# Attention and the later stages in one block, with the first two shared pairs between attention's last steps

## What is computed

```
h = h + attn(layernorm(h))          # gated attention unit: silu(x @ uv_w) -> u, v, q, k
                                    # relu(q k^T + w_rel)^2 @ v, times u, @ o_w, + x * res_scale
t = layernorm(h)
shared = sum over 2 experts of gelu(t @ sw1 + sb1) @ sw2, + sb2
cw     = softmax(t @ gate_w + gate_b), kept for the top 2 of 8 experts
routed = sum over 8 experts of cw * (gelu(t @ rw1 + rb1) @ rw2 + rb2)
out = h + shared + routed
```

## Time and profile before

| | us |
|---|---|
| median of three runs | 1364.53 |
| profiled execution | 1364.89 |
| its span | 1363.1 |
| TensorE busy | 1231.9 (90%) |
| VectorE busy | 1009.1 (74%) |
| GpSimd busy | 830.3 (61%) |
| ScalarE busy | 827.3 (61%) |

### The profile page before, as it was taken

How to read it: one execution, slowest core, us unless ns; L and a number is a source line. 1 busy time by engine, 2 the same in 40 slices (tenths; PEclk the granted TensorE clock), 3 DMA queues, 4 the chain that set the end, 5 groups by cost and what they waited for, 6 DMA issues and landing times.

```text
span 1363.1 us, 39403 instructions
## 1 busy us (share of the span) xinstructions
PE 1231.9 (90%) x11910; PEld 1010.8 (74%) x11911; DVE 1009.1 (74%) x2599; ACT 827.3 (61%) x1969; POOL 830.3 (61%) x824
## 2 busy tenths in 40 slices
PE   4999999999999998257999989999999999998997
PEld 2777877777777886235777778888888888966676
DVE  3688788778788787238777757777777777789997
ACT  1566566565656665153444447777777777756664
POOL 3345776676767765667777616676676676753331
PEclk7999999999999999668999999999999999999999
DMA  5233334343333312124444222222222322236663
GB/s 153 81 126 112 116 117 128 100 132 114 120 113 125 127 60 69 61 81 132 121 115 119 73 57 81 83 84 81 82 84 76 86 81 80 64 99 179 187 179 106
DMA packets 119520, 142.62 MB, mean 105 GB/s; under 512 B 18591, under 2 KB 98782, under 8 KB 119417
## 3 DMA queue, kind: packets, MB, share of 16 engines
q1 hardware_dynamic: 95800, 101.42, 25.6%
q0 software_dynamic: 19584, 33.45, 8.1%
q10 hardware_dynamic: 4032, 6.57, 1.9%
HBM read 86.38 MB, written 55.96 MB: 104 GB/s over the span
## 4 chain that ended last, share of the span: by engine, by line
PE 45%; DVE 7%; issue 3%; ACT 2%; DMA 0%; POOL 0%; DVEq 0%; ACTq 0%
PE bank L1615 4%; PE bank L1637 4%; PE bank L1636 4%; PE bank L1638 4%; PE bank L1616 4%; PE bank L1617 4%; PE bank L1081 3%; PE bank L1080 3%; PE bank L1079 3%; PE bank L1033 2%; PE bank L1034 2%; DVE hid_all L1062 2%; PE bank L1035 2%; DVE hid_all L1064 2%; PE bank L1603 2%
## 5 line engine op out<-in xcount | busy, mean ns | idle before, releaser
L1334 POOL DMA_INDIRECT y_dram<-y_sb,y_row x244 | 273.1, 1119 | 154.5 <-issue 74.5
L1041 ACT ACTIVATE gel_all<-bank,b 128x458 f32<-128x458 f32 x256 | 157.1, 641 | 161.8 <-PE bank L1035 148.5
L1411 ACT ACTIVATE gel_all<-bank,b 128x256 f32<-128x256 f32 x488 | 192.9, 473 | 54.1 <-PE bank L1617 30.3
L1081 PE MATMUL bank<-w_hi,hid_all 128*117 128x128 f16 (+1 forms) x1024 | 181.5, 221 | 0.0
L1080 PE MATMUL bank<-w_lo,hid_all 128*117 128x128 f16 (+1 forms) x1024 | 181.4, 221 | 0.0
L1079 PE MATMUL bank<-w_hi,hid_all 128*117 128x128 f16 (+1 forms) x1024 | 181.4, 221 | 0.0
L1636 PE MATMUL bank<-w_hi,hid_all 128*128 x976 | 173.1, 220 | 0.0
L1637 PE MATMUL bank<-w_lo,hid_all 128*128 x976 | 170.5, 219 | 0.0
L1638 PE MATMUL bank<-w_hi,hid_all 128*128 x976 | 170.5, 219 | 0.0
L1534 DVE CAST hid_all<-gel_all 128x1024 f16<-128x1024 f32 x122 | 85.4, 700 | 103.3 <-ACT gel_all L1411 103.3
L1323 POOL DMA_INDIRECT slots_dram<-rows_s,slot_2nd x128 | 133.6, 1044 | 39.6 <-issue 38.3
(11 more groups left out here) (185 smaller groups left out, 3266.8 us busy)
## 6 DMA issues: line engine op xcount, KB each, us to landing
xin<-in_xmain SPq DMA_DIRECT2D x32, 771.8 KB
rows_r<-slots_dram SPq DMA_DIRECT2D x122, 130.0 KB
x2r_dram<-rows_1st SPq DMA_DIRECT2D x32, 260.0 KB, 2.6
rows_s<-x2r_dram SPq DMA_DIRECT2D x32, 260.0 KB, 2.7
scratch<-y_dram SPq DMA_DIRECT2D x32, 234.0 KB
x2t_dram<-x2T SPq DMA_DIRECT2D x32, 229.0 KB, 2.9
scratch<-y_dram SPq DMA_DIRECT2D x32, 224.0 KB
x_cols<-x2t_dram ACTq DMA_DIRECT2D x28, 229.0 KB, 2.7
```

The source lines that it names most:

```text
L1081: last = pe.matmul(dst, lo, self.w_hi[:, w], start=False, stop=f == self.NG - 1)
L1334: pool.indirect_dma_start(out=y_dram, in_=y_sb[:, s, c, :], in_offset=None, out_offset=bass.IndirectOffsetOnAxis(ap=y_row[:, s, c:c + 1], ...
L1411: act.activation(gel[:, s8 % 2, f, :], up_bank[s8 % 2][half][:, (f % 2) * TILE:(f % 2 + 1) * TILE], ACT.Gelu, bias=b1[:, bass.ds((e + SHAR ...
```

## The change

Both functions now return their engines' programs and one block calls them, attention's first. All semaphores live to the end; `Done` hands attention's to the later stages. `ones`, `b2`, `x_cols`, `slot_1st` and the four row buffers are allocated outside both functions, and the buffers of the shared pairs lie over those of attention that are free by then.

After steps 30, 31 and 32 `steps` calls a function `between`. SyncE loads the columns of pairs 0 and 1 after step 30. After step 31 TensorE, ScalarE and VectorE do `up`, `gelu` and `split` of pair 0; after step 32, pair 1 with the `down` of pair 0. Pair 0 uses three PSUM banks in turn, and VectorE splits it like the others. The meeting of the engines and SyncE's waits between the blocks are gone; `load_rows(0)` to `(3)` wait for attention's scatter and store from the same buffer instead. `tag_rows` moves back by one pair (rows 2i-2 and 2i-1 in pair i), the fill tails go behind `load_rows(16)`, the tables are computed in three parts behind pairs 3, 4 and 5, and the memset of `scratch` goes from VectorE to GpSimd. The b2 work goes to attention's start: loads behind `rel`, sums and casts on GpSimd at the end of step -2. The experts' PSUM banks are renumbered.

```diff
-        def steps(eng, step):
+        def steps(eng, step, between=None):
...
             for i in range(hi, PAIRS + 4):
                 step(i, i % 2, i // 2, i % 4)
+                if between is not None and i >= PAIRS - 2:
+                    between(eng, i)
...
-            for parity in range(2):
-                sp.wait_ge(t_out[parity], 16 * PAIRS // 2)
-            for buf in range(ROW_BUFS):
-                sp.wait_ge(r_out[buf], 16 * PAIRS // ROW_BUFS)
-                sp.wait_ge(scattered[buf], 64 * PAIRS // ROW_BUFS)
-            sp.wait_ge(w_late, 16)
...
+            def sum_biases():
+
+                own = Own(pool, b2_up)
+                s0, s1 = EXPERTS * HID, (EXPERTS + 1) * HID
+                own.did(pool.memset(b2[:, :], 0.0))
+                pool.wait_ge(b2_loaded, 64)
+                own.did(pool.tensor_tensor(b2_in[:, s0:s1], b2_in[:, s0:s1], b2_in[:, s1:B2_COLS], ALU.add))
+                own.wait()
+                own.did(pool.tensor_copy(b2[0:B2_LO, :], b2_in[0:B2_LO, 0:s1]))
+                own.wait()
+                own.did(pool.tensor_copy(b2_high[B2_LO:, :], b2_in[B2_LO:, 0:s1]))
+                own.wait()
+                own.did(pool.tensor_tensor(b2[B2_LO:2 * B2_LO, :], b2_in[B2_LO:, 0:s1], b2_high[B2_LO:, :], ALU.subtract))
...
+                if isinstance(i, int) and i == -2:
+                    sum_biases()
...
+    def up_free(self, pe, k, f):
+
+        if self.before is not None and isinstance(k, int) and k < 2 and f < (3 if k == 0 else 4):
+            if k == 0:
+                pe.wait_ge(self.before.sil, 5 * PAIRS)
+            else:
+                pe.wait_ge(self.gel_ready, self.NG)
+                pe.wait_ge(self.before.mid_ready, PAIRS)
+        elif self.before is not None and isinstance(k, int) and k == 0:
+            pe.wait_ge(self.gel_ready, f - 2)
+        elif not (isinstance(k, int) and k == 0 and f < 4):
+            pe.wait_ge(self.gel_ready, self.NG * k + f - 3)
...
+        def sync_between(sp, i):
+            if i == PAIRS - 2:
+                for k in range(2):
+                    sp.wait_ge(done.t_out[k], 16)
+                    early.load(sp, k, k)
...
                 if i >= ROWS_BUFS:
                     sp.wait_ge(scattered[b], 64 * (i // ROWS_BUFS))
+                else:
+                    sp.wait_ge(done.scattered[b], 64 * PAIRS // ROW_BUFS)
+                    sp.wait_ge(done.r_out[b], 16 * PAIRS // ROW_BUFS)
...
             for i in range(PAIRS):
                 load_rows(i)
-                if i == 6:
+                if i == 16:
                     sp.wait_ge(tables_up, 3)
...
+            pool.memset(scratch[:, 1024:], 0.0).then_inc(scratch_up, 1)
...
+        def scalar_between(act, i):
+            if i == PAIRS - 1:
+                act.wait_ge(done.w_late, 16)
+                for f in range(NG):
+                    early.gelu(act, 0, f)
+                act.wait_ge(done.t_out[0], 32)
+                early.load(act, 2, 0)
+            if i == PAIRS:
+                for f in range(NG):
+                    early.gelu(act, 1, f)
+                act.wait_ge(done.t_out[1], 32)
+                early.load(act, 3, 1)
...
-                        tag_rows(2 * i, 2 * q % ROWS_BUFS)
+                        tag_rows(2 * i - 2, (2 * q + 2) % ROWS_BUFS)
...
             tag_rows(0, 0)
             tag_rows(1, 1)
-            for i in range(1, EARLY_PAIRS):
+            for i in range(2, EARLY_PAIRS):
...
+        def vector_between(dve, i):
+            if i == PAIRS - 1:
+                for j in range(NJ):
+                    early.split(dve, 0, 0, j)
+            if i == PAIRS:
+                vector_pair(dve, 1, 1)
...
+        def tensor_between(pe, i):
+            if i == PAIRS - 1:
+                pe.wait_ge(done.ws_done, PAIRS)
+                for f in range(NG):
+                    early.up(pe, 0, 0, f)
+            if i == PAIRS:
+                pe.wait_ge(done.b2_up, B2_STEPS)
+                tensor_pair(pe, 1, 1)
```

More of the change, by code:

```diff
@@ L15 @@
+from collections import namedtuple
 from contextlib import ExitStack
@@ L58 @@
 B2_LO = 32
+B2_COLS = (EXPERTS + SHARED) * HID
+B2_STEPS = 5
 EARLY_PAIRS = 18
@@ L72 @@
 TINY = 1e-30
+Done = namedtuple("Done", "t_out r_out scattered ws_done top_kept slots_up mid_ready sil x2T_ready routed lg_read w_late b2_up")
 class Own:
@@ new lines, in build @@
+        slot_1st = sbuf("slot_1st", [P, 2, GROUP], U32)
+        attend, done = embed_and_attend(
+            nc, keep, bank, acc, w_hi, w_lo, b1, ident, top8, slot_2nd, tag_2nd, region_at, next_at, ones, b2, row_bufs, slot_1st,
+            xmain, xrest, tokw_main, tokw_rest, txt, tokb, token, pos, emb2, emb3, emb4, w_rel, uv_w, o_w, gamma, beta, g, res,
+            gate_w, gate_b, ffn_w, ffn_b1, shared_b2, routed_b2, x2t_dram, x2r_dram, slots_dram)
+        experts = experts_and_combine(
+            nc, keep, done, bank, acc, w_hi, w_lo, b1, ident, top8, slot_2nd, tag_2nd, region_at, next_at, ones, b2, x_cols,
+            row_bufs, x2t_dram, x2r_dram, slots_dram, y_dram, out)
@@ new lines, in build, with _ @@
+        block = keep.enter_context(nc.Block())
+        @block.sync
+        def _(sp):
+            attend["sync"](sp, experts["sync_between"])
+            experts["sync"](sp)
+        @block.gpsimd
+        def _(pool):
+            attend["gpsimd"](pool)
+            experts["gpsimd"](pool)
+        @block.vector
+        def _(dve):
+            attend["vector"](dve, experts["vector_between"])
+            experts["vector"](dve)
+        @block.scalar
+        def _(act):
+            attend["scalar"](act, experts["scalar_between"])
+            experts["scalar"](act)
@@ L461, in _, with vector @@
             steps(pool, step)
-        @block.vector
-        def _(dve):
+        def vector(dve, between):
             own = Own(dve, setup_v)
@@ L701, in _, with scalar @@
                                      op0=ALU.mult, op1=ALU.subtract).then_inc(uvw_ready, 1)
-            steps(dve, step)
-        @block.scalar
-        def _(act):
+            steps(dve, step, between)
+        def scalar(act, between):
             act.wait_ge(w_in, 16 * N_W)
@@ L819, in step, with tensor @@
                     weights_hi(i, p)
-            steps(act, step)
-        @block.tensor
-        def _(pe):
+            steps(act, step, between)
+        def tensor(pe, between):
             def text(grp):
@@ L998, in _ @@
             pe.wait_ge(setup_v, 9)
-            steps(pe, step)
+            steps(pe, step, between)
+    done = Done(t_out, r_out, scattered, ws_done, top_kept, slots_up, mid_ready, sil, x2T_ready, routed, lg_read, w_late, b2_up)
+    return {"sync": sync, "gpsimd": gpsimd, "vector": vector, "scalar": scalar, "tensor": tensor}, done
 class SharedExperts:
@@ L1005, with __init__ @@
     NJ = NG // 2
-    def __init__(self, nc, ctx, tag, first, flip, bank, acc, w_hi, w_lo, b1, b2, ones, x_cols, gel, hid, x2t_dram):
+    def __init__(self, nc, keep, tag, first, flip, up_bank, down_bank, acc, w_hi, w_lo, b1, b2, ones, x_cols, gel, hid, x2t_dram,
+                 before=None):
         def sem(name):
-            return ctx.enter_context(nc.semaphore(f"{name}_{tag}"))
+            return keep.enter_context(nc.semaphore(f"{name}_{tag}"))
         self.first, self.flip, self.acc, self.x2t_dram = first, flip, acc, x2t_dram
@@ L1018, in __init__, with up_dst @@
         self.acc_done = sem("acc_done")
+    def up_dst(self, k, f):
+        lead = self.before is not None and isinstance(k, int) and k == 0
+        return self.up_bank[f % 3 if lead else f % 4][:, 0:PAIR_SEQ]
+    def up_free(self, pe, k, f):
[9 more added lines that the diff above has]
+            pe.wait_ge(self.gel_ready, self.NG * k + f - 3)
     def load(self, eng, k, parity):
@@ L1090, in accumulate, with experts_and_combine @@
                           ALU.add).then_inc(self.acc_done, 1)
-def experts_and_combine(nc, bank, acc, w_hi, w_lo, b1, ident, top8, slot_2nd, tag_2nd, region_at, next_at,
-                        shared_b2, routed_b2,
-                        x2t_dram, x2r_dram, slots_dram, y_dram, out):
+def experts_and_combine(nc, keep, done, bank, acc, w_hi, w_lo, b1, ident, top8, slot_2nd, tag_2nd, region_at, next_at, ones, b2,
+                        x_cols, row_bufs, x2t_dram, x2r_dram, slots_dram, y_dram, out):
     LAG, AHEAD = 2, 2
```

253 lines of the change are left out of this document (103 added, 150 removed).

## The result

The changed kernel takes 1354.11 us (median of 4: 1352.51, 1355.85, 1354.86, 1353.37), the kernel before 1364.57 (4 runs). The ratio is 0.9926, 95% interval 0.9909 to 0.9944. In a later comparison, with six runs, it was 1355.91 against 1365.00, ratio 0.9924 (0.9909 to 0.9939). Ratios and their intervals rest on the executions within 1.5% of a kernel's fastest; this leaves out only four of the twelve of experiment 4, the profiled one among them. The sign was right; the predicted 1341.0 and its range, 1334 to 1350, were not.

What follows compares the result with a forecast made beforehand. TensorE was taken as the bound after the seam's holes. Of its chain (transposes at 773.1) and GpSimd's (775.9), the later decides: against 799.67 a gain of 23.8, kept as 23.5, from 1364.53 to 1341.0 us, range 1334 to 1350.

Steps and rivals of the forecast that it cites:

- What bounds the kernel: Between attention and shared pairs, GpSimd's queue, a barrier and a load leave TensorE idle 24.23 us; afterwards TensorE is the bound.
- pair 0: First shared pair: up-projections start at 554.0 in an idle gap, delaying ScalarE's rows of pair 31 by 5 us to 563.4.
- pair 1 before rank(15): On TensorE pair 1 runs ahead of rank(15), ending at 581.4; slots are up at 583.3 where they were at 567.3.
- GpSimd to the first tag: Last first-choice scatters, fill and row loads put tags at 597.9; TensorE stops some 12 us before resuming near 600.0.
- Set-up: nothing: Bias work moved to the start takes GpSimd 7.6 us, delaying it 2.7, covered by 4.8 us before the first reader.
- Rival B: Row ring slips at load_rows(17) behind the fill tails: 1 to 2 us lost once, repeated 5 to 9; 1346 to 1350, chance 0.16.
- E: Rival: shared pairs slower throughout as TensorE trails GpSimd's four row buffers, 15x for x us per pair; 1371 at 2.0, chance 0.04.
- The GpSimd chain, 172 us: The 128 second-choice scatters run from 598.1 to 770.1, 172 us as before; landing and a tile load put transposes at 775.9.
- The sum: The later chain decides when the routed tiles' transposes start: 775.9 against 799.67, a gain of 23.8 us, kept as 23.5.
- the forecast's own signs: Forecast wrong if rank comes before 578 or after 586, pairs' pace differs from 10.57, or transposes are over 5 us from 776.

Runs made afterwards that it cites:

- experiment 4: Changed kernel with one fill tail behind each of row loads 16 to 23, in place of all eight behind row load 16: 1363.78 us, ratio 0.9957.
- experiments 1 and 2: Changed kernel with the b2 bias casts and subtraction cut to 1 column, then whole but in nine pieces over three steps: 1349.81 and 1350.06 us.
- Experiment 5: Changed kernel with seven row buffers in place of four, fill tails left where they are: 1348.87 us, ratio 0.9869.
- experiment 7: Changed kernel with seven row buffers, expert tables behind pairs 13 to 15 and fill tails behind the last row load: 1347.97 us, ratio 0.9886.

## Why the prediction was wrong, step by step

**What bounds the kernel, pair 0, pair 1 before rank(15):** right. Taken 3.9 us later as a whole, they come where they were put, within 1.5 us: pair 0 at 557.9 (554.0), ScalarE's rows at 566.95 (563.4), rank at 583.89 (581.4), slots at 586.4 (583.3). One part was left out and is hidden: a table load of 1.28 us stands ahead of pair 0's first GELU, at 558.76. VectorE's tables behind the pairs hide as said in pairs 3 to 5, 10.57 us each, and then cost TensorE 0.9 us: pairs 6 and 7 take 11.0.

**GpSimd to the first tag:** right in order and nearly in size. First tag at 602.1 (597.9), table load 1.28 us as taken by the trace, and the GELU starts behind it without a gap, so the Trainium skill's further 1.38 us of drain ("ScalarE: Activation LUTs", "What ACT_TABLE_LOAD costs") are not seen here either: the tag ends at 603.23, the load runs from 603.25 to 604.53, and the GELU starts at 604.54. The first row loads landed 3.9 us after their issue; 2.7 had been taken.

**Set-up: nothing.** The step that failed first. GpSimd's own time was overrated and its effect on front_powers was hidden, as said. I asked who waits for GpSimd's queue, and not whom GpSimd's instructions slow down while they run. It costs some 4 us, shown by experiments 1 and 2. The Trainium skill has a rule for it ("SBUF — State Buffer", "Who interferes with whom"): VectorE and GpSimd share a pair of SBUF ports, which VectorE needs in its two-port modes, `tensor_scalar` among the instructions that can enter them; whichever instruction issues first has the pair to its end, and the other waits. I had not weighed it. The trace agrees: three of xn's four instructions end 0.1 us behind the end of one of GpSimd's, the last of them at 44.45, behind the subtraction's 42.01 + 2.35 = 44.36.

**Rival B's "Against: the load is due about when the fills end, so 1 to 2 us are lost once", and E's "a buffer's round is ... well under the 21 us of four batches".** The step that failed most: a slip of 12.4 us in place of 0 in the forecast and 1 to 2 in B. Both sentences count from the scatter that frees a buffer to the tag that fills it again, and take for granted that the scatters keep up with the tags. They took 1.18 us where before they took 1.04 on average, fell 6 us back within five pairs, and used up the ring before the fill tails came. The mechanism is E's, its price B's upper end and more; in the profile it ends with the stop at the fill tails. Experiment 5 shows the ring's part, experiment 7 that of the tables.

**The GpSimd chain, 172 us.** 175.8 without the slip, 178.4 with it. The working had the warning in hand, 172.0 against 161, and put part of the 11 us to the fill tails. In the trace of before GpSimd waits only 1.3 us for tags; the rest is scatters longer than those of the earlier trace rows, four steps of which make 5.1 us: batches 4 to 6, counted from 0, beside and behind the tables, take 6.8, 7.7 and 5.8 us, the others 5.1 to 5.5. There TensorE waits 6.6 us between 625 and 634, so GpSimd loses no ground to it, and is in step from 645 on. Hiding the tables took that pause away. That is the second half of the same step: a duration read in one arrangement was carried to another.

The sum goes up: 775.9 + 3.9 for the set-up + 3.8 for the pace give 783.6, where the transposes stand with seven buffers (783.37); both terms are read from the traces, so this closes the account and forecasts nothing. The ring adds 7 to 10 (790.76 and 793.71 in the two profiles of the changed kernel). Of the forecast's own signs, rank came between 578 and 586, while the pace of the pairs and the date of the transposes both failed.

## What to carry to other kernels

Where two engines feed each other through a small ring, compare their free paces before comparing the ring's round trip: an engine that is a tenth slower for 60 us (5.9 us a batch against 5.3) uses up 6 us of slack, and then holds the faster one. And when work is moved beside another engine's, its price is also what the neighbour's instructions lose; look up how long they take in stretches with and without such company. Last, a duration that is longer than its parts (172 against 161) is to be explained from the trace before it is carried over.

## What the runs showed of the hardware

- VectorE's tensor_scalar over 128 columns, four of them: 1.12 us alone, 1.55 to 1.61 us beside GpSimd's 128-column pieces, 2.52 to 5.12 us beside its memset, casts and subtraction of 1152 columns, by how many of these they meet.
- The issue of an indirect DMA on GpSimd takes 0.94 us at best and up to 1.89 us beside VectorE's casts and subtractions. The scatter at 668.04, 1.73 us long, ends at 669.77, 0.12 us behind VectorE's cast:

```profile
669.02 0.63 DVE L1115 CAST hid_all<-gel_all 128x916 f16<-128x916 f32 x1
```

  Overlap alone is not the measure: in step, 85 scatters take 1.00 us on average though VectorE is busy for seven tenths of the time. Which moment within the issue is sensitive stays open.
- GpSimd can run in step with the shared pairs though it waits for nothing (0.30 us between all scatters): with seven buffers its batches take 5.12 and 5.45 us in turn, 10.57 together, and over 19 of them each starts 3.79 to 3.81 us behind the start of ScalarE's latest tag; in the changed kernel 5.05 and 5.13 us in turn.
- One chip gave 1524 us for the kernel before at one time and 1365 later; between 640 and 790 us the kernel with seven buffers has dozens of gaps on TensorE that the trace lays to no wait, up to 1.5 us long, in its profile of the first time, and one in that of the second. Nothing here says why.
